# Summing the states by transposes that add into PSUM, in a bidirectional selective-scan block with soft mixture of experts

## The reference

```python
dA_cum = exp(flip(cumsum(flip(dA_shift))))            # per position, channel (512) and state (16)
xs = cumsum(dB_u * dA_cum) / (dA_cum + 1e-12)
y = einsum('bldn,bln->bld', xs, C)                    # the sum over the 16 states
y = flip(y) if reverse; y = y + u * D                 # the skip term
return y * silu(res)
...
y = ssm(xf, res) + ssm(xb, res, reverse=True)
return y @ out_proj_w.T
```

## Time and profile before

| | |
|---|---|
| median of 3 runs | 7026.24 us |
| span of the profiled execution, first to last instruction | 7017.1 us |
| what lies around the span (median less span) | 9.1 us |
| one pass of the sequence loop | 365 us (DVE busy 339, PE 280, POOL 262, ACT 252) |
| mean granted TensorE clock | 0.885 of 2.4 GHz over the span, 0.86 in the loop |

### The profile page before, as it was taken

One profiled execution on the slowest core, in us unless ns is written; L12 is line 12 of the kernel. 1 busy time (PEld: TensorE's weight loads), 2 busy tenths in 40 slices (PEclk: granted clock), 3 DMA queues, 4 the chain that ended last, 5 costly groups with the idle time before them and its releaser, 6 DMA issues. The chain is left out here.

```text
span 7017.1 us, 79490 instructions
## 1 busy us (share of the span) xinstructions
PE 5452.5 (78%) x14584; PEld 2611.9 (37%) x14584; DVE 5767.6 (82%) x8375; ACT 4186.0 (60%) x6495; POOL 4206.1 (60%) x3210
## 2 busy tenths in 40 slices
PE   5777777777777777878786877777777777899978
PEld 2333333333333333333333333333333333556566
DVE  7999999989999999999999999999999998222223
ACT  4767676666767676767676767676767665211100
POOL 3767777777777776767676767676777775000000
PEclk8988888888888888889898989898988898999989
DMA  2333333333333333333342423333333332322355
GB/s 76 115 99 113 102 111 102 109 103 107 106 104 105 107 103 110 108 99 116 95 121 90 122 91 119 94 115 99 114 100 112 102 109 79 93 87 87 92 187 203
DMA packets 554755, 755.05 MB, mean 108 GB/s; under 512 B 123584, under 2 KB 272064, under 8 KB 552192
## 3 DMA queue, kind: packets, MB, share of 16 engines
q1 hardware_dynamic: 554240, 750.73, 34.7%
HBM read 660.80 MB, written 89.75 MB: 107 GB/s over the span
## 5 line engine op out<-in xcount | busy, mean ns | idle before, releaser
L963 PE MATMUL y_ps<-v_ring,ident 128*128 128x512 f32 x4096 | 2388.9, 689 | 858.9 <-POOL v_ring L513 304.3
L504 POOL TENSOR_TENSOR g_ring<-dtu,b_ring 128x512 f32<-128x512 f32 x2048 | 2726.3, 1350 | 40.1 <-DMA b_ring<-bc_scr 27.5
L808 DVE TENSOR_TENSOR_SCAN s_ring<-e_ps,g_ring 128x512 f32<-128x512 f32 x2048 | 2478.8, 1210 | 80.8 <-POOL g_ring L504 80.8
L513 POOL TENSOR_TENSOR v_ring<-z_ring,c_ring 128x512 f32<-128x512 f32 x1024 | 1296.1, 1266 | 1599.3 <-DVE z_ring L816 1599.2
L616 ACT ACTIVATE e_ps<-dt,a_neg 128x512 f32<-128x512 f32 x2048 | 1408.7, 688 | 1084.6 <-DVE s_ring L808 1078.6
L630 ACT ACTIVATE f_ps<-rsum,guard_bias,a_neg_half 128x512 f32<-128x512 f32 x2048 | 1572.0, 768 | 30.9 <-DVE z_ring L816 30.3
L963 PEld LDWEIGHTS y_ps<-v_ring,ident 128*128 128x128 f32 x4096 | 775.2, 212 | 2008.9 <-issue 881.3
L816 DVE SCALAR_TENSOR_TENSOR f_ps<-f_ps,s_ring 128x512 f32<-128x512 f32 x1024 | 707.6, 691 | 229.5 <-ACT f_ps L630 186.3
L816 DVE SCALAR_TENSOR_TENSOR z_ring<-f_ps,s_ring 128x512 f32<-128x512 f32 x1024 | 696.1, 680 | 92.3 <-ACT f_ps L630 92.2
L825 DVE TENSOR_TENSOR v_ring<-f_ps,c_ring 128x512 f32<-128x512 f32 x1024 | 679.1, 663 | 0.0
L896 PE MATMUL side<-u,conv_diag 128*128 128x512 f32 x1056 | 489.6, 607 | 41.6 <-ACT disp_ring L597 41.6
(11 more groups left out here) (123 smaller groups left out, 5728.4 us busy)
## 6 DMA issues: line engine op xcount, KB each, us to landing
b_ring<-bc_scr SPq DMA_DIRECT2D x1024, 256.0 KB, 3.2
c_ring<-bc_scr SPq DMA_DIRECT2D x1024, 256.0 KB, 3.2
pT_scr<-rowT_ring SPq DMA_DIRECT2D x136, 256.0 KB, 3.6
m_pT<-pT_scr SPq DMA_DIRECT2D x16, 2048.0 KB, 8.3
sT_scr<-sT_ring SPq DMA_DIRECT2D x272, 64.0 KB, 2.4
x_xT<-sT_scr SPq DMA_DIRECT2D x16, 1024.0 KB, 8.9
eo_scr<-x_eo SPq DMA_DIRECT2D x32, 512.0 KB, 5.1
m_eo<-eo_scr SPq DMA_DIRECT2D x16, 1024.0 KB, 10.8
```

The source lines that it names most:

```text
L504: pool.tensor_tensor(g_ring[:, t % 4], dtu[d][:, c], b_ring[:, k], ALU.mult).then_inc(g_done, 1)
L513: pool.tensor_tensor(v_ring[:, t % VR], z_ring[:, t // 2 % 3], c_ring[:, RING[t // 2]], ALU.mult).then_inc(v_odd, 1)
L808: dve.tensor_tensor_scan(flip(s_ring[:, t % 3]), flip(e_ps[:, t % 2]), flip(g_ring[:, t % 4]), 0.0, ALU.mult, ALU.add).then_inc(scan_done, 1)
L963: pe.matmul(y_ps[:, t % 2], ident[:], v_ring[:, t % VR], start=(state_of(t) == 0), stop=True, skip_group_check=True).then_inc(v_used, 1)
```

## The change

The sum over the states is turned round. For each tile PE now takes the four 128x128 blocks of v as stationary operands, with the identity moving, in transpose mode, and adds the four results into `y_ps`: positions are on the partitions. The skip terms become four products of 128x128 with u as the stationary operand. `y_out` writes into a new buffer `yT` (positions on the partitions, 512 channels). Four new side jobs `y_0` to `y_3` turn it back, by four transposes each, and DVE multiplies each by `res_gate` straight from PSUM into `yg` at lag 2; `y_gate` is gone. `out_0` waits until y_2 and y_3 have been read. The timetable gets the four jobs and begins with conv1_0; its first half is laid out anew, and the norm starts at tile 18 instead of 14. The second half, from tile 64 on, is as it was.

```diff
     order = """
-        res0 conv1_0 out0 out1 out2 out3 conv1_1 res1 conv1_2 res2 conv1_3 res3 x1_0 dt1_0 dt1_1 xnT0 xnT1
+        conv1_0 y0 y1 y2 y3 res0 out0 out1 out2 out3 conv1_1 res1 conv1_2 res2 conv1_3 res3 x1_0 dt1_0 dt1_1 xnT0 xnT1
         rows0 rows1 dt1_2 cols0 cols1 rowsT0 rowsT1 dt1_3 colsT0 colsT1 slots0 slots1
...
-WEIGHT = {"out": 2.0, "res": 3.4, "conv0": 5.2, "conv1": 5.2, "x0": 4.4, "x1": 4.4, "dt0": 5.0, "dt1": 5.0, "in0": 2.2,
+WEIGHT = {"y": 1.4, "out": 2.0, "res": 3.4, "conv0": 5.2, "conv1": 5.2, "x0": 4.4, "x1": 4.4, "dt0": 5.0, "dt1": 5.0, "in0": 2.2,
           "xnT": 0.8, "rows": 3.3, "cols": 3.4, "rowsT": 1.0, "colsT": 1.0, "slots": 2.2}
...
 PROLOGUE = ("in0", "conv0", "x0", "dt0")
-EPILOGUE = ("out", "xnT", "rows", "cols", "rowsT", "colsT", "slots")
+EPILOGUE = ("y", "out", "xnT", "rows", "cols", "rowsT", "colsT", "slots")
...
-    NORM_TILE = 14
+    NORM_TILE = 18
     CR = 256
...
         conv_tanh, res_tanh = dt, dtu[1]
+        yT = sb("yT", [P, LT, DI])
         yg = sb("yg", [P, KI, L])
...
         v_even, v_odd, v_used = sem("v_even"), sem("v_odd"), sem("v_used")
-        y_evac, yg_done = sem("y_evac"), sem("yg_done")
+        y_evac = sem("y_evac")
         chain, x1_done, xn_normed = (
...
                 d = int(kind[-1]) if kind[-1] in "01" else None
-                if lag == 2 and kind not in ("out", "cols"):
+                if lag == 2 and kind not in ("y", "out", "cols"):
                     act.wait_ge(side_done, at.done(s))
...
+            dve.memset(yT[:], 0.0)
             dve.memset(yg[:], 0.0)
...
                 src, free = side[:, at.bank(s)], side_free[at.bank(s)]
+                if kind == "y" and lag == 2:
+                    dve.wait_ge(side_done, at.done(s))
+                    dve.tensor_tensor(yg[:, i], src, res_gate[:, i], ALU.mult).then_inc(free, 1)
                 if kind == "out" and lag == 2:
...
-                pair = slice(0, 2) if part in (1, 3) else slice(2, 4)
+                pair = slice(0, 2 * P) if part in (1, 3) else slice(2 * P, 4 * P)
+                rows = y_ps[:].rearrange("p h (t d) -> p (h t) d", d=2 * P)
                 if part in (1, 2):
-                    dve.tensor_copy(yg[:, pair], y_ps[:]).then_inc(y_evac, 1)
+                    dve.tensor_copy(yT[:, :, pair], rows).then_inc(y_evac, 1)
                 else:
-                    dve.tensor_tensor(yg[:, pair], y_ps[:], yg[:, pair], ALU.add).then_inc(y_evac, 1)
-            def y_gate(at, part):
-                pair = slice(0, 2) if part == 3 else slice(2, 4)
-                dve.wait_ge(y_evac, at.seq(1) * 4 + (part + 1))
-                dve.tensor_tensor(yg[:, pair], yg[:, pair], res_gate[:, pair], ALU.mult).then_inc(yg_done, 1)
+                    dve.tensor_tensor(yT[:, :, pair], rows, yT[:, :, pair], ALU.add).then_inc(y_evac, 1)
...
                         y_out(at, part)
-                    if t % SEG == 3 and part in (0, 3):
-                        y_gate(at, part)
                     norms(t, 0)
...
             y_out(epi, 0)
-            y_gate(epi, 0)
             for s in EPI:
...
             pe.sem_inc(v_used, CR)
+            def rows_of(lb, q):
+                return y_ps[:, lb // 2, (lb % 2 * 2 + q) * P:(lb % 2 * 2 + q + 1) * P]
...
                     mm = pe.matmul(bank, w_dt[:, d, i * P:(i + 1) * P], xdbl[0:R], start=True, stop=True)
+                elif kind == "y":
+                    if i == 0:
+                        pe.wait_ge(y_evac, at.seq(1) * 4 + 1)
+                    for t in range(LT):
+                        mm = pe.transpose(bank[:, t * P:(t + 1) * P], yT[:, t, i * P:(i + 1) * P], ident[:])
                 elif kind == "out":
                     if i == 0:
-                        pe.wait_ge(yg_done, at.seq(1) * 2 + 1)
+                        for c in range(KI - 2, KI):
+                            read("y", c)
                     for c in range(KI):
...
                             pe.wait_ge(v_odd, t0_half + (t // 2 + 1 + CR))
-                        pe.matmul(y_ps[:, t % 2], ident[:], v_ring[:, t % VR], start=(state_of(t) == 0), stop=True,
-                                  skip_group_check=True).then_inc(v_used, 1)
+                        for lb in range(LT):
+                            mm = pe.matmul(rows_of(lb, t % 2), v_ring[:, t % VR, lb * P:(lb + 1) * P], ident[:], is_transpose=True,
+                                           start=(state_of(t) == 0 and t % 2 == 0 and lb % 2 == 0), stop=True,
+                                           skip_group_check=True)
+                        mm.then_inc(v_used, 1)
                     for d, q, pair in SKIPS.get(t, ()):
-                        pe.matmul(y_ps[:, q], d_diag[:, d, 2 * pair + q], u[d][:, 2 * pair + q, PAD:],
-                                  start=False, stop=True, skip_group_check=True)
+                        for lb in range(LT):
+                            pe.matmul(rows_of(lb, q), u[d][:, 2 * pair + q, PAD + lb * P:PAD + (lb + 1) * P],
+                                      d_diag[:, d, 2 * pair + q], start=False, stop=True, skip_group_check=True)
                     for s in range(SLOTS):
...
     }
-    nc = bacc.Bacc("TRN2", target_bir_lowering=False, num_devices=1)
+    nc = bacc.Bacc("TRN2", target_bir_lowering=False, num_devices=1, dynamic_dma_scratch_size=1024)
     arrays, aps = {}, {}
```

## The result

| | before | after |
|---|---|---|
| median, runs side by side | 7025.51 us (4 runs, 7019.71 to 7026.32) | 7061.05 us (4 runs, 7059.46 to 7062.88) |
| ratio to before | | 1.0053, 95% interval 1.0038 to 1.0067 |
| span of the profiled execution | 7017.1 us | 7060.4 us |
| one pass of the sequence loop | 364.9 us | 367.5 us |
| mean granted TensorE clock | 0.885 | 0.797 |

The kernel became slower by 35 us; 7049 was forecast, and the range holds it. The pass is taken between the first guards of the first and the last pass, a fifteenth of it each. It grew by 2.6 us; forecast was 1.3. By the traces the growth is 16 x 2.6 = 42 us, 7 more than the medians differ. The profiled execution of after took 7061.96 us, 1.6 more than its span. In every execution on record with both numbers the time is 1.5 to 1.7 us more than the span.

A forecast was written before the change was run, and what follows sets the result against it. DVE was taken as the bound, busy 339.2 of 365.2 us a sequence. Terms summed to +1.3 us a pass, +21 over 16 passes, plus 2 for the epilogue: 7026 + 23 = 7049 us, range 6975 to 7125.

The forecast's parts named there:

- conv0_0: Conv job at tile 74, ahead of guard 77: shorter v clears PE's backlog, so the lateness goes, -1.88 us a pass.
- conv1_1: Conv job at tile 14, waiting for out_2's bank: guard 17 late by 2.2 instead of 1.3, +0.9 us a pass.
- res_0: Job at tile 9, waiting for y_2's bank: just hidden at 2.4 GHz, 1.5 late at 1.2 GHz; +0.8 us a pass.
- x1: Job at tile 27, ahead of guard 30: never late before, now late by 0, 1.0 or 2.8 us; +1.0 a pass.
- x0: Job that keeps its place, ahead of guard 96: later because PE will be idler ahead of it, +0.5 us a pass.
- The accumulating transposes: Four transposes of v adding into PSUM: taken as 0.44 us, no dearer than others; bounds 0.44 and 0.86.
- the loop's clock: Granted PE clock in the sequence loop: expected to be 0.7 to 0.8 in place of 0.86.
- It adds to DVE 0.15: DVE's own work: four gates out of PSUM instead of two, +0.15 us a pass, bounds 0 and +0.4.
- conv0_3 likewise: Conv job at tile 88, ahead of guard 91: gains from shorter v like conv0_0, -0.6 of its 1.49 us lateness.
- The Ln steps and the row exponentials: ACT's steps that shift by up to four tiles: net effect put at nothing, +-1 us a pass.
- PE's busy time: PE busy in one pass: to fall from 280 to between 190 and 230 us.
- Rival C: PE stays at 1.2 GHz outside the convs: +9.5 us a pass, 7180 us; chance 0.12.

The follow-up runs named there:

- the kernel with the places alone: The kernel before, with its product and gates, but its jobs at the changed kernel's tiles and the norm from tile 18: 7056.48 us, ratio 1.0047.
- the kernel with products: The changed kernel with the four blocks of v as fp32 products with the identity instead of transposes: 7110.56 us, ratio 1.0123.

## Why the prediction came out as it did

**What held.** The direction: PE was busy 37 us less in a pass and the end came later. conv0_0 had a backlog ahead of it and kept its place, and its 1.88 us went. conv1_1 began behind DVE's release of the bank at the full clock (3.70 us) and left guard 17 late by 2.02 in each pass; 2.2 was forecast, and the kernel with the places alone has the same 2.02, so this is the place and not the clock. res_0 took 3.78 us for four records in the pass shown, as four of v do at 1.2 GHz in the earlier trace rows; x1 took 6.63 there, and its guard was 1.54 late on average, between my values of 1.0 and 2.8. The places alone made 1.17 of that. x0 lost the half microsecond. The accumulating transposes cost as much as the others: a group of four every 0.43 us at the full clock (1983.03 and 1983.46 above; 0.44 in the earlier trace rows). Guards 12, 17 and 30 were late, as the forecast needed, and the loop's clock of 0.77 is within 0.7 to 0.8.

**What failed.** Three terms of the sum and one number. The single terms missed by more than the sum: those that came out above their forecast (DVE's own work, conv0_3, x1, res_0) did so by 3.1 us a pass together, those below (the Ln steps, conv0_2, conv1_0, conv1_1) by 2.1. That only 1.1 is left of them is luck.

"It adds to DVE 0.15" was 1.3. The gates were 0.25 of it; I had looked at what DVE runs and not at what GpSimd runs beside it. The rest came with the places: with them alone, DVE's work grew by 1.5, mostly in scans that come second behind GpSimd (18 us in the whole trace, 1.1 a pass). I had put the effect of the shift at nothing.

"conv0_3 likewise", -0.6, was +0.39. The timeline of before has this job behind a wait for its bank:

```profile
2164.62 5.40 PE L896 MATMUL side<-u,conv_diag 128*128 128x512 f32 x8 [2.60 <-ACT disp_ring L597]
```

There was no backlog for v to shorten, and the bracket of that row would have told me. What it lost is the clock: in before it took 5.40 us in 8 of the 16 passes and 3.70 in the other 8, with guard 91 late by 1.49 and 0.58; in after it took 5.1 to 5.4 in all of them. And 1.49 was the worse half of the passes, not the typical one.

The Ln steps and the row exponentials, put at nothing within 1, gave 1.31 back: the waits of 0.46, 1.34 and 2.01 a pass at guards 32, 38 and 44 became 1.33 at guard 42 and 0.35 at guard 50, and those at guards 57 (56 in before) and 62 rose by 0.8 together.

PE's busy time of 190 to 230 us in a pass was too low. The transposes of v took 1512 / 16 = 94.5 us and not 56. The 56 was 128 times the 0.44 us after which the next instruction can follow, but a group of four that stands alone counts as 0.60 us busy or more; and some 30% of the groups ran at 1.2 GHz, 1.1 us each. That cost nothing by itself.

**The clock and the transposes.** Rival C was 7180 us, with a loop near 0.65. The loop stood at 0.77, and eight transposes a tile instead of four brought the whole from 0.797 to 0.877, as the earlier trace rows had it. The Trainium skill, TensorE: Matmul & The Clock Gate, section "Part 4: PE-mode transpose", says that the full clock does not engage for transposes; these runs do not agree with it.

## What to carry to other kernels

Before you price a faster operation, read the bracket ahead of each job that someone waits for, and in all passes: behind a backlog the job gains, behind a wait it gains nothing and pays for a lower clock. When a change moves jobs by a tile or two, the places are an edit of their own and may outweigh it; run them alone, and retime both kernels before you judge the operation. A wait can also be removed by putting work into it that has to be done in any case.

## What the runs showed of the hardware

With less work on PE the granted clock was lower, 0.885 in before and 0.797 in after, and work that had not changed took longer: the products of the conv jobs 489.6 us in all in before and 535.1 in after, those of x 143.4 and 187.2. Four fp32 transposes of 128x128 with their weight loads took 0.43 us at the full clock, also while they add. Four fp32 products of that shape took 1984.27 - 1983.38 = 0.89 us, eight records; in the kernel with products:

```profile
1983.38 1.05 PE L973 MATMUL y_ps<-ident,v_ring 128*128 128x128 f32 x8
1984.27 1.89 PE L920 MATMUL side<-w_out,yg 128*128 128x256 f32 x8
```

DVE's scan of a row and GpSimd's products, both in SBUF alone, did not run at once: where they met, the later one took 2.31 or 2.06 us, and a start 0.03 us apart settled which one that was.
